# Expert token weights through DRAM, and counted zero products on TensorE, in a two-layer vision tower with two mixtures of experts

## The reference

```python
h = patches @ w + b; h = concat(cls_tok, h)
h = h + attention0(layernorm(h))      # no softmax: s*s + s
h = h + experts0(layernorm(h))        # 8 experts of width 768, the best 2 of each token
h = h + attention1(layernorm(h))      # 12 heads, 8-bit fake quantisation, integer softmax
h = h + experts1(layernorm(h))        # 8 experts of 128, 8 of 256, the best 8 of each token
# experts: out += comb[:, e] * (gelu(x @ w1_e) @ w2_e), comb normalised over the chosen
```

## Time and profile before

| | |
|---|---|
| median of three runs | 398.92 us (397.49 to 399.99) |
| the profiled execution | 398.0 us, its span 396.2 us |
| mean granted clock of TensorE over the span | 0.822 |
| PE, DVE, ACT, POOL busy | 74%, 69%, 54%, 6% of the span |
| expert layer 0, expert layer 1 | about 66 to 193 us, 318 to 387 us |

### The profile page before, as it was taken

One profiled execution on the slowest core, in us unless ns is written; L12 is line 12 of the kernel. 1 busy time (PEld: TensorE's weight loads), 2 busy tenths in 40 slices (PEclk: granted clock), 3 DMA queues, 4 the chain that ended last, 5 costly groups with the idle time before them and its releaser, 6 DMA issues.

```text
span 396.2 us, 5821 instructions
## 1 busy us (share of the span) xinstructions
PE 294.4 (74%) x2160; PEld 271.0 (68%) x2160; DVE 272.6 (69%) x729; ACT 213.4 (54%) x528; POOL 23.6 (6%) x46
## 2 busy tenths in 40 slices
PE   5849958889999999999655034069620678999992
PEld 5737837789999999999555013048420568999991
DVE  1166264488888888888647997985368368888862
ACT  0034435676876876877344457570010658888860
POOL 7010000000000000000000004800000000000000
PEclk9968975999999999999958555559555569999997
DMA  8950300030330330200000000000500001221001
GB/s 236 286 206 0 139 2 0 1 135 8 140 140 2 140 141 2 93 2 0 2 1 0 0 2 0 0 2 0 185 0 1 2 0 36 74 95 78 2 2 40
DMA packets 8475, 21.71 MB, mean 55 GB/s; under 512 B 1136, under 2 KB 2784, under 8 KB 8448
## 3 DMA queue, kind: packets, MB, share of 16 engines
q1 hardware_dynamic: 7872, 20.39, 15.0%
q0 software_dynamic: 576, 0.96, 1.1%
HBM read 20.95 MB, written 0.40 MB: 54 GB/s over the span
## 4 chain that ended last, share of the span: by engine, by line
PE 65%; DVE 21%; ACT 6%; issue 3%; DMA 2%; SPq 1%; ACTq 0%; DVEq 0%
PE bank L539 25%; PE bank L608 8%; PE bank L523 8%; PE bank L591 4%; PE bank L589 4%; PE bank L511 2%; DMA embed_area<-w_tok_dram 2%; PE bank L806 2%; PE bank L720 2%; PE bank L582 2%; DVE bn L1149 1%; DVE embed_area L1477 1%; PE bank L791 1%; PE bank L803 1%; ACT hid_hi L941 1%
## 5 line engine op out<-in xcount | busy, mean ns | idle before, releaser
L539 PE MATMUL bank<-hid_hi,pj_parts 128*128 128x260 f32 x288 | 76.0, 285 | 1.9 <-DVE hid_lo L1253 1.8
L941 ACT ACTIVATE hid_hi<-hidden_area 128x260 fp32r<-128x260 f32 x144 | 55.1, 422 | 38.4 <-DVE hidden_area L1248 38.4
L1248 DVE TENSOR_TENSOR hidden_area<-hidden_area 128x260 f32<-128x260 f32 x144 | 55.4, 424 | 15.2 <-ACT hidden_area L932 7.3
L1253 DVE TENSOR_TENSOR hid_lo<-hidden_area,hid_hi 128x260 fp32r<-128x260 f32 x144 | 55.8, 427 | 10.9 <-ACT hid_hi L941 1.4
L539 PEld LDWEIGHTS bank<-hid_hi,pj_parts 128*128 128x128 f32 x288 | 54.1, 188 | 2.7 <-DVE hid_lo L1253 1.9
L934 ACT ACTIVATE hidden_area<-bank 128x260 f32<-128x260 f32 x144 | 48.3, 382 | 5.1 <-PE bank L591 4.9
L539 PE MATMUL bank<-xt_hi,fc_hi 128*128 128x260 f32 x144 | 42.5, 295 | 3.9 <-issue 3.8
L591 PE MATMUL bank<-xt_lo,fc_lo 128*128 128x260 f32 x144 | 42.3, 294 | 0.0
L589 PE MATMUL bank<-xt_lo,fc_hi 128*128 128x260 f32 x144 | 41.8, 290 | 0.0
L539 PE MATMUL bank<-xt_lo,fc_hi 128*128 128x260 f32 x144 | 41.7, 290 | 0.0
L539 PE MATMUL bank<-xt_hi,fc_lo 128*128 128x260 f32 x144 | 41.6, 289 | 0.0
(11 more groups left out here) (301 smaller groups left out, 561.5 us busy)
## 6 DMA issues: line engine op xcount, KB each, us to landing
raw_area<-fc_dram SPq DMA_DIRECT2D x8, 768.0 KB, 4.3
raw_area<-pj_dram SPq DMA_DIRECT2D x8, 576.0 KB, 5.4
raw_area<-fc_dram SPq DMA_DIRECT2D x6, 512.0 KB, 4.1
raw_area<-pj_dram SPq DMA_DIRECT2D x6, 384.0 KB, 4.5
embed_area<-patches_dram SPq DMA_DIRECT2D x8, 256.0 KB, 4.6
embed_area<-w_tok_dram SPq DMA_DIRECT2D x8, 96.0 KB, 6.7
score_area<-w_l_dram SPq DMA_DIRECT2D x1, 576.0 KB, 11.0
attn_area<-w_qkv_dram POOLq DMA_DIRECT2D x1, 432.0 KB, 6.8
```

Source lines behind the costliest of these rows:

```text
L539: mm = pe.matmul(out, lhs[a], rhs[b], start=start and n == 0, stop=stop and n == 2, skip_group_check=True)
L941: act.activation(hid_hi[:, x % 3, tok], hid_w[:, x % 2, tok], ACT.Copy).then_inc(hid_hi_ready[y], 1)
L1248: dve.tensor_tensor(hid_w[:, x % 2, tok], hid[:, x % 2, tok], tok_w_b[:, tiles[x].expert % 2, tok], ALU.mult).then_inc(weighted[y], 1)
L1253: dve.tensor_tensor(hid_lo[:, x % 3, tok], hid_w[:, x % 2, tok], hid_hi[:, x % 3, tok].bitcast(F32), ALU.subtract).then_inc(hid_lo_ready[y ...
```

## The change

The weights of one expert of the first layer and two of the second (`MADE`) are still made by a pick product, now in plain float32 from `comb_t` (no high and low parts, `comb_r` and `row_pick_r` are gone, and with them two VectorE instructions a layer). For all other experts ("turns"), SyncE writes `comb_t` to DRAM once a layer (`comb_to_dram`), waits for it, and reads each expert's row back to all 128 partitions (`token_weights`, 266,240 bytes each), 7 in the first layer and 14 in the second, into four buffers: the two of before and two in `xn`. They are queued between the loads. VectorE waits for the transfer at an expert's first tile. In the second layer the wide experts now come first.

`fill(n)` issues n products of bf16 zeros (128 x 128 by 128 x 260) on TensorE into a bank that is otherwise unused there: 44 behind the embedding, 28 ahead of `transpose_x(1)`, 34 ahead of `transpose_x(2)` and 16 behind it.

```diff
-        comb_r = sb("comb_r", [128, NT, 2 * E1], F32R)
-        comb_t = sb("comb_t", [128, B * S], F32R)
+        xn_words = xn[:].rearrange("p i d -> p (i d)")
+        tok_w = [tok_w_b[:, 0], tok_w_b[:, 1], xn_words[:, 0:B * S], xn_words[:, B * S:2 * B * S]]
+        comb_t = sb("comb_t", [128, B * S])
         row_pick = sb("row_pick", [128, E0 + E1])
-        row_pick_r = sb("row_pick_r", [128, E0 + E1], F32R)
+        zeros = sb("zeros", [128, HALF], BF16)
+        comb_dram = [nc.dram_tensor(f"comb{y}_dram", (n, B * S), F32).ap() for y, n in enumerate((E0, E1))]
...
+        MADE = (1, 2)
...
+        TILES = [[Tile(0, x // T0, x // T0, x % T0 == 0, x // T0, x % T0) for x in range(E0 * T0)],
+                 [Tile(1, 8 + x // 2, x // 2, x % 2 == 0, E0 + x // 4, x % 4) for x in range(16)]
+                 + [Tile(1, x - 16, x - 8, True, E0 + x // 4, x % 4) for x in range(16, 24)]]
...
-                order += [("w", tiles[x].expert)] * tiles[x].first + [("h", x)]
+                order += [("w", tiles[x].turn)] * (tiles[x].first and tiles[x].made) + [("h", x)]
...
+            def comb_to_dram(y):
+                sp.wait_ge(comb_t_ready, 2 * (y + 1))
+                sp.dma_start(comb_dram[y], comb_t[0:(E0, E1)[y], :]).then_inc(comb_out, 16)
+                sp.wait_ge(comb_out, 16 * (y + 1))
+
+            def token_weights(y, turn):
+
+                if turn >= 4:
+                    sp.wait_ge(weighted[y], 2 * first_tile(y, turn - 3))
+                row = TILES[y][first_tile(y, turn)].expert
+                sp.dma_start(tok_w[turn % 4], comb_dram[y][row].partition_broadcast(128)).then_inc(tok_w_in[turn % 4], 16)
+
+            def load0(n):
                 sp.wait_ge(w_lo_done[n % 2], 4 * (n // 2))
                 load(n % 2, t["fc0"][n], t["pj0"][n], T0)
-            for n in range(6):
+
+            def load1(n):
                 sp.wait_ge(w_lo_done[n % 2], 4 * ((E0 + n) // 2))
                 if n == 1:
 
                     sp.wait_ge(pv_cls_mm, 1)
                     sp.wait_ge(e_ready, len(CHUNKS))
-                load(n % 2, t["fc1"][n], t["pj1"][n], 4)
+                load(n % 2, t["fc1"][(n + 2) % 6], t["pj1"][(n + 2) % 6], 4)
+
+            load0(2)
+            comb_to_dram(0)
+            for turn in range(1, 4):
+                token_weights(0, turn)
+            load0(3)
+            for n in range(4, E0):
+                token_weights(0, n)
+                load0(n)
+            for n in range(3):
+                load1(n)
+            comb_to_dram(1)
+            for turn in range(MADE[1], E1):
+                token_weights(1, turn)
+                if turn in (4, 6, 8):
+                    load1(turn // 2 + 1)
...
+            def fill(n):
+
+                for _ in range(n):
+                    pe.matmul(PB[7][:, 0:HALF], zeros[:, 0:128], zeros[:], start=True, stop=True, skip_group_check=True)
...
-                    out = PB[2][0:2 * n_exp, i * 128:(i + 1) * 128] if i < 4 else PB[3][0:2 * n_exp, 0:B]
-                    last = pe.transpose(out, comb_r[0:n, i, 0:2 * n_exp].bitcast(F32), ident[0:n, 0:n])
+                    out = PB[2][0:n_exp, i * 128:(i + 1) * 128] if i < 4 else PB[3][0:n_exp, 0:B]
+                    last = pe.transpose(out, (comb0, comb1)[layer][0:n, i, :], ident[0:n, 0:n])
...
-                            e = x + (0, E0)[y]
-                            mm = pe.matmul(out, row_pick_r[:, e:e + 1].broadcast_to([128, 128]), comb_t[:, tok],
+                            e = tiles[first_tile(y, x)].expert + (0, E0)[y]
+                            mm = pe.matmul(out, row_pick[:, e:e + 1].broadcast_to([128, 128]), comb_t[:, tok],
                                            start=True, stop=True)
...
+            pe.wait_ge(zeros_ready, 1)
+            fill(44)
             pe.wait_ge(consts_in, 80)
             transpose_x(0)
...
+            fill(28)
             transpose_x(1)
             gate(1, w_gate0, E0)
             wait_split_x(1)
             ffn(0, E0)
             turn_back(0)
 
+            fill(34)
             transpose_x(2)
+            fill(16)
             wait_split_x(2)
...
-                            act.activation(tok_w_b[:, x % 2, tok], src, ACT.Identity).then_inc(entry_out[y], 1)
+                            act.activation(tok_w[x % 4][:, tok], src, ACT.Identity).then_inc(entry_out[y], 1)
...
-                then(dve.tensor_tensor(out[:], ch, rinv[:].unsqueeze(2).broadcast_to([128, NT, n]), ALU.mult))
-
-                then(dve.tensor_copy(comb_r[:, :, 0:n], out[:]))
-                dve.tensor_tensor(comb_r[:, :, n:2 * n], out[:], comb_r[:, :, 0:n].bitcast(F32),
-                                  ALU.subtract).then_inc(comb_ready, 1)
+                dve.tensor_tensor(out[:], ch, rinv[:].unsqueeze(2).broadcast_to([128, NT, n]),
+                                  ALU.mult).then_inc(comb_ready, 1)
...
-                    k = max(ENTRIES[y].index(("h", x)), ENTRIES[y].index(("w", tiles[x].expert)))
+                    tile, k = tiles[x], ENTRIES[y].index(("h", x))
+                    if tile.made:
+                        k = max(k, ENTRIES[y].index(("w", tile.turn)))
+                    elif tile.first:
+                        dve.wait_ge(tok_w_in[tile.weights], 16 * weights_from_dram(y, tile.turn))
                     for n in range(2):
 
                         tok = slice(n * HALF, (n + 1) * HALF)
                         dve.wait_ge(entry_out[y], 2 * k + n + 1)
-                        dve.tensor_tensor(hid_w[:, x % 2, tok], hid[:, x % 2, tok], tok_w_b[:, tiles[x].expert % 2, tok],
+                        dve.tensor_tensor(hid_w[:, x % 2, tok], hid[:, x % 2, tok], tok_w[tile.weights][:, tok],
```

More of the change, by code:

```diff
@@ L273, in build @@
         xlo_ready = sem("xlo_ready")
-        row_pick_ready = sem("row_pick_ready")
+        comb_t_zero = sem("comb_t_zero")
+        zeros_ready = sem("zeros_ready")
+        comb_out = sem("comb_out")
+        tok_w_in = [sem(f"tok_w_in{k}") for k in range(4)]
         entry_mm = [sem(f"entry_mm{n}") for n in range(2)]
@@ L382, in build, with __init__ @@
         PAIRS = [(0, 1), (6, 7)]
+        MADE = (1, 2)
         class Tile:
-            def __init__(self, expert, first, load, j, last):
-                self.expert, self.first, self.load, self.j, self.last = expert, first, load, j, last
+            def __init__(self, y, expert, turn, first, load, j):
+                self.expert, self.turn, self.first, self.load, self.j = expert, turn, first, load, j
                 self.slot = load % 2
+                self.weights = turn % 4
+                self.made = turn < MADE[y]
         LOAD_TILES = [T0] * E0 + [4] * 6
         LOADS = len(LOAD_TILES)
-        TILES = [[Tile(x // T0, x % T0 == 0, x // T0, x % T0, x % T0 == T0 - 1) for x in range(E0 * T0)],
-                 [Tile(x, True, E0 + x // 4, x % 4, x % 4 == 3) for x in range(8)]
-                 + [Tile(4 + x // 2, x % 2 == 0, E0 + x // 4, x % 4, x % 4 == 3) for x in range(8, 24)]]
+        TILES = [[Tile(0, x // T0, x // T0, x % T0 == 0, x // T0, x % T0) for x in range(E0 * T0)],
+                 [Tile(1, 8 + x // 2, x // 2, x % 2 == 0, E0 + x // 4, x % 4) for x in range(16)]
+                 + [Tile(1, x - 16, x - 8, True, E0 + x // 4, x % 4) for x in range(16, 24)]]
         ENTRIES = []
         for tiles in TILES:
-            order = [("h", 0), ("h", 1), ("w", 0)] + [("w", tiles[1].expert)] * tiles[1].first
+            order = [("h", 0), ("h", 1), ("w", 0)]
             for x in range(2, len(tiles)):
-                order += [("w", tiles[x].expert)] * tiles[x].first + [("h", x)]
+                order += [("w", tiles[x].turn)] * (tiles[x].first and tiles[x].made) + [("h", x)]
             ENTRIES.append(order)
@@ L407, in entries_of, with first_tile, weights_from_dram @@
             at = order.index(("h", x))
-            return order[at - 1:at + 1] if TILES[y][x].first else order[at:at + 1]
+            return order[at - 1:at + 1] if TILES[y][x].first and TILES[y][x].made else order[at:at + 1]
+        def first_tile(y, turn):
+            return next(x for x, tile in enumerate(TILES[y]) if tile.turn == turn)
+        def weights_from_dram(y, turn):
+            earlier = [(0, n) for n in range(MADE[0], E0)] + [(1, n) for n in range(MADE[1], E1)]
+            return sum(n % 4 == turn % 4 for _, n in earlier[:earlier.index((y, turn)) + 1])
         def tiles_to(y, load):
@@ L618, in ffn @@
                 pe.wait_ge(comb_t_ready, 2 * (y + 1))
-                if y == 0:
-                    pe.wait_ge(row_pick_ready, 3)
                 entry("w", 0)
-                if tiles[1].first:
-                    entry("w", tiles[1].expert)
                 for x in range(len(tiles)):
@@ L1301, in _ @@
             settle(dve.memset(logits[:], 0.0))
-            then(dve.memset(zeros[:], 0.0))
-            for n in range(2):
-                dve.tensor_copy(comb_t[:, n * HALF:(n + 1) * HALF], zeros[:]).then_inc(row_pick_ready, 1)
```

(5 more changed lines are left out.)

10 lines of the change are left out of this document (3 added, 7 removed).

## The result

The changed kernel takes **389.38 us** (median of 4 executions, 386.67 to 391.5) against 399.09 for the kernel before (4 executions). The ratio is 0.974, with a 95% interval of 0.969 to 0.979: faster by 2.6%. The forecast was 386.8 us with a range of 381.5 to 392.5. The profiled execution took 390.48 us (span 388.7), 7.5 us less than the 398.0 on which the prediction's sum was made; the sum had 12.1.

What follows compares the result with a forecast made beforehand. TensorE's products were taken to bound the expert layers; elsewhere it waits, then runs at half clock. Gains 3.9 + 1.0 + 2.7 + 4.5 = 12.1 us off 398.0 give 385.9, plus 0.9 for the median: 386.8 us, range 381.5 to 392.5.

Steps and rivals of the forecast that it cites:

- the sum: Whole kernel: the gains of the three turnings' fills and the expert layers added up, 12.1 us off the profiled 398.0.
- Embedding fill: 44 zero products behind the embedding: transposes, then query/key products at full clock, 3.9 us saved; bounds 2.2 and 4.1.
- The rival that zeros do not hold the clock: At the fills: the clock falls where it did, leaving only the expert layers' gain; 398.5 us, chance 0.07.
- Second turning: 28 zero products ahead of it: 0.4 us at transposes, 0.6 at gates before the clock falls; 1.0 us saved.
- The rival in which the clock holds through the gates: Behind the second turning: full clock kept throughout the gates, 3.4 us more saved, 383.4 us; chance 0.18.
- Third turning: 34 and 16 zero products: projection at full clock, bound passing to VectorE's 12 reductions, 2.7 us saved; bounds 0.9 and 3.1.
- Expert layers: Pick products cut from 48 to 6 in both layers: 4.5 us saved; bounds 3 and 5.
- Transfers hidden: Expert layers: the token weight broadcasts land before they are needed, no cost; late-landing rival 394.4 us, chance 0.06.
- The other rivals: Including: the clock also drops for a time at the embedding or third-turning fills, 389 to 391 us, chance 0.14.
- The rival on the slower side: Clock already at half when each fill starts, fills overrun their waits: 8 us slower, 407 us, chance 0.05.

Runs made afterwards that it cites:

- experiment 6: Changed kernel with the 44 zero products behind the embedding replaced by 66 float32 ones of 65 columns, 128 rows and 96 output partitions: 394.26 us, ratio 0.989.
- experiment 10: Changed kernel with the 44 zero products behind the embedding replaced by 28 float32 ones of 65 rows, 96 output partitions and 65 columns: 389.03 us.
- experiment 4: Changed kernel with 34 instead of 28 zero products ahead of the second turning, 6 behind its transposes and 15 behind the gates: 389.34 us, ratio 0.968.
- experiment 11: Changed kernel with 14 wide zero products between and behind the attention's narrow ones, ahead of the output projection: 387.13 us, ratio 0.967.
- experiment 5: Changed kernel with zero products at four more waits: ahead of the output projection, around the fourth turning, behind the second layer's gates: 385.99 us, ratio 0.968.
- experiment 7: Changed kernel with 20 more instructions (redundant waits) in SyncE's program ahead of the third expert's weights: 388.06 us, ratio 0.969.
- experiment 9: Changed kernel with experiment 5's second-layer fills, experiment 7's SyncE program, 120 zero products ahead of the score rows, fourth value product moved earlier: 385.96 us, ratio 0.964.
- experiment 12: Experiment 9 with the 14 zero products of experiment 11 added: 385.84 us, ratio 0.965.

## Why the prediction was right, and where it was off

**Embedding fill, 3.9 us.** 0.85 and 3.09 measured, and the same in the fills alone. 44 products took 5.04 us, 0.115 each. The rival that zeros do not hold the clock is out; experiments 6 and 10 show that it depends on the form of the product.

**Second turning, 1.0 us.** It gave 2.4: 0.35 at the transposes, 1.65 at the gates and 0.41 in the wait behind. The mechanism was as forecast: small products let the clock fall in spite of the fill, at 61.8 us. Only the moment was off: I had 57.4 to 59.8, and of the 2.2 us that full speed gives the gates 1.65 were kept, not 0.6. The moment is not fixed: that stretch took 4.68 to 4.83 us in five profiles with this fill and 5.07 to 5.53 in five others. The rival in which the clock holds through the gates is wrong even with every pause filled (experiment 4). The Trainium skill's section "Why this matters for your kernels" of "TensorE: Matmul & The Clock Gate" names idle gaps alone; here 3.40 us of 3.40 busy were followed by half clock, so the rows decide against reading it as the only cause.

**Third turning, 2.7 us.** 0.79 + 2.22 - 0.29 = 2.7. The twelve reductions start at 201.73 and start 0.60 apart, the last at 208.35, so the bound did pass to VectorE:

```profile
201.73 0.69 DVE L1409 TENSOR_REDUCE stat_q<-attn_area 96x1 f32<-96x520 f32 x1 [1.99 <-ACT attn_area L1067]
...
208.35 0.68 DVE L1410 TENSOR_REDUCE stat_q<-attn_area 96x1 f32<-96x520 f32 x1
```

**Expert layers, 4.5 us.** 1.65 + 3.17 + 0.09 = 4.9, all of it in the run with the transfers alone.

**Transfers hidden.** The DMA issues of after: a token weight transfer of 260 KB lands in 3.4 or 3.6 us, less than the 5.4 of the earlier trace rows or the 7.2 us there was; VectorE never waits for one. From the write of the weights to the first issue of a broadcast, the round trip through memory, 1.5 us pass (71.81 to 73.33).

```profile
xn<-comb_dram SPq DMA_DIRECT2D x12, 260.0 KB, 3.4
hidden_area<-comb_dram SPq DMA_DIRECT2D x9, 260.0 KB, 3.6
...
71.81 0.34 SPq L447 DMA_DIRECT2D comb_dram<-comb_t  x1
73.33 0.33 SPq L455 DMA_DIRECT2D hidden_area<-comb_dram  x1
```

**The other rivals.** The clock did not fall at the first place in any of nine profiles with fills of 260 columns there, nor at the third in any of eleven. The rival on the slower side needed half clock at each fill's start; only the second fill ever met it, where the clock had fallen in the output projection (0.35 to 0.5 us late).

**What the sum lacked.**
- *That the profile of before was a lucky one.* Its embedding ended at 19.01 us and its output projection ran at full clock. In the second profile of before these are 20.45 us and 6.87, and in the twelve of the other kernels 18.66 to 22.38 us, and 3.61 to 6.87. They are 3.7 and 3.3 us of scatter that no fill here governs (those of experiment 11 may). The score rows and products of the second layer are a third such stretch, with 3.0 us (experiments 4 and 5). Together they are large enough for the 3 to 7 us by which one kernel's executions mostly differ, but only the profiled ones can be split up. The step that failed is the one that takes 12.1 us off one execution: 398.0 was 1.6 to 3.2 us below the medians of before in the later comparisons (399.6 to 401.2), and the forecast gave back only 0.9 of that.
- *The tail.* I had costed SyncE's longer program by what its issues delay and had nothing for its length. It is 23 instructions longer, and an 8 KB piece is fetched while the outputs are issued. The tail is 0.7 to 1.0 us longer in every kernel with the transfers, and this is gone in the three whose SyncE program is longer still (experiments 7, 9 and 12), where the second expert layer has one fetch more on that queue instead. A further 1.0 to 1.4 us came in two profiles of the same program, each time with a 16 KB fetch on another queue beside the third issue, which took 1.91 and 1.61 us instead of 0.60. In the twelve other profiles there was neither. The coincidence holds in all fourteen, but no run moved that fetch alone: experiment 7 lacks it with TensorE's program unchanged, and why is open.

So the first result lies in the range partly by luck: the foreseen stretches gave 14.0 us, not 12.1, and the tail took back 0.7 to 2.1 that the sum did not have.

The stretches thus say 14.0 us, less 0.7 to 2.1 in the tail: 12 to 13. By the medians after is 9.7, 10.9 and (experiment 7, without the loss in the tail) 11.6 us below before; the ratios 0.974, 0.969 and 0.969 make that 10.5, 12.3 and 12.5 us, each to within about 2. That agrees with the stretches within the noise (for experiment 7 they say 14.0). How the scatter of the three stretches falls in each execution was not measured.

## What to carry to other kernels

Compare kernels stretch by stretch between landmarks, with several profiles of each, before a difference in one is put down to the change: here two stretches differed by over 3 us between profiles in which their work was the same, and a third lost 3 us in two profiles of twelve. A fill of zero products in a wait is worth what the work behind it gains at full speed, provided that the fill covers the wait and is made of a form that held the clock (here 260 columns and 128 rows), and that what follows is not itself a run of small products. A tail that is issued one transfer after the other should be looked at for instruction fetches when the issuing engine's program grows.

## What the hardware showed

- A TensorE that the record shows busy without a pause can still lose its clock. 56 passes of 65 rows, 96 partitions and 65 columns let it fall 3.9 us after their start; 132 passes of 128 rows, 96 partitions and 65 columns held it for 11.35 us. The clock fell behind or among the attention's outputs (65 rows), the gates (8 columns) and the products of 12 columns, at moments that differ between executions: 16.3 us into the score rows and products in experiment 9, 11.5 in experiment 12, the same work in both. In experiments 4, 5 and 12 it fell within 0.2 us of the start of 12 products of 68 columns over all 128 rows, with the 12-column ones still to come, so 65 rows or 12 columns are not the whole account; what else counts is open.
- With wide products strewn among narrow ones (8 of 260 columns among 64 passes, and 6 in the wait behind) it stayed at 1.00 in two profiles of two; without them it did so in three of twelve.
- In after the clock is 1.00 again at 259.8 us, when TensorE, idle for 17.89 us until 254.27, has since run nothing but 20 transposes (the last begins as the clock rises) and, in 8 passes, 4 products of 128 columns and 6 output partitions; the first of these groups:

```profile
254.72 1.49 PE L842 MATMUL bank<-ident,score_area 128*128 128x128 f32 x6
256.14 0.60 PE L845 MATMUL bank<-ident,score_area 128*6 128x128 f32 x4
```

  The Trainium skill, "TensorE: Matmul & The Clock Gate", section "Part 4: PE-mode transpose", says that transposes do not engage the full clock; this rise disagrees with it.
- A longer SyncE program went with a longer tail. With 23 instructions more, in eight profiles of eight, an 8 KB instruction fetch of 0.3 to 0.5 us stands in the tail, the last output issue starts 0.4 us behind the end of the one before it, and the tail is 0.7 us longer or more. With 20 more still, in three of three, fetch, gap and loss are gone.
